# The dense experts of the first layer in two passes over the tokens

## The chip, the cores and the metric

One core of a Trainium2 chip runs the whole program. The metric is device time in microseconds (us), the median of three runs of the kernel. The profile is of one more execution.

## What is computed

4096 tokens (32 samples of 128, width 128, float32) go through two layers; each is a conditioning mixture of experts, a feed-forward part and a residual. The part that matters here is the feed-forward part of the first layer, in which all eight experts run on every token ("dense"):

```python
g = jnp.einsum('bsh,ehf->ebsf', x, w_gate)      # 8 experts, 128 -> 512
u = jnp.einsum('bsh,ehf->ebsf', x, w_up)
h = jax.nn.silu(g) * u
expert_out = jnp.einsum('ebsf,efh->ebsh', h, w_down)
cw = router_probs * gate_weights                # per token and expert
cw = cw / (jnp.sum(cw, axis=-1, keepdims=True) + 1e-09)
out = jnp.einsum('ebsh,bse->bsh', expert_out, cw)
```

The second layer's conditioning part then needs, for each token, the top two of eight router scores of the finished first layer, before its routed experts can be weighted.

## The kernel before

Tokens lie on the free axis in 8 blocks of 512 columns (`BLK`, `NBLK`). Products keep near-float32 precision by splitting both operands into a high part (float32r) and a rest: high x high, low x high, high x low, so three matmuls for each product.

The order of work is one list, `plan()` (lines 91 to 124), of items; the place k of an item is its slot. Kinds: A (shared expert, first layer's conditioning), G (its routed groups), **B** (the dense experts), S and R (shared and routed experts of the second layer), F (its last part). A B item is one block, one expert, one quarter f of the 512 hidden columns; there are 8 experts x 8 blocks x 4 = 256, expert outermost (lines 100 to 102). All engines walk the same slots in order, and every side job is pinned to a slot by a dictionary.

For a B item at slot k, TensorE (PE) multiplies gate and up into two PSUM banks of a ring of four (`up`, lines 917 to 951, six matmuls), and in the same slot does the three down matmuls of the item LAG = 5 slots earlier (`down`, lines 953 to 994). ScalarE (ACT) computes Silu of the gate bank (line 1078). VectorE (DVE) multiplies it with the up bank into `Hf` (line 1551). ACT copies that into the high part `HH` (line 1084), one slot later; DVE, or for every fourth item GpSimd (POOL), subtracts to get the rest `HL` (lines 1571 and 1663). When a block of an expert is done (four items), DVE multiplies its result with the token weights in `CWB` into `TMP` (line 1425), and POOL adds that to the tokens in `XT` (line 1678).

**Expert weights.** `ST` holds two raw experts (`fill_b`, DMA of 768 KB from SyncE's queue, lines 726 on). The split buffers are `WBH`/`WBL`, two of each. `split_wb` pins three pieces of 512 columns for each expert: DVE casts a piece into `WBH` (line 1498), POOL computes the rest `WBL` (line 1605). Piece 0 is gate, 1 is up, 2 is down. The slots, counted from the first slot of an expert, `first_b[ex]`:

```python
first_b = [pos["B", 0, ex, 0].k for ex in range(8)]
fill_b = {pos["G", 8, 0, 0].k: 0, first_b[0] + LAG + 10: 1}
fill_b |= {first_b[ex - 1] + 2: ex for ex in range(2, 8)}
split_wb = {t + 7 + k: (ex, k) for t, ex in fill_b.items() if ex for k in range(3)}
c0 = first_b[1] + LAG + 12
fill_c = {c0: 0, c0 + 1: 1, c0 + 4: 2, c0 + 6: 3}
split_wc = {c0 + 2: (0, 0), c0 + 3: (0, 512), c0 + 4: (1, 0), c0 + 5: (1, 512)}
```

So expert 1 is split at slots 22 to 24 after the first B item, and expert ex at slots 9 to 11 of expert ex - 1, whose pass over the blocks has 32 slots. TensorE waits for each piece in block 0's first item (lines 934 to 936, 984 to 991). `split_wc` splits the second layer's weights in the same way (line 1504) while expert 1 runs, fed by `fill_c`.

**Token weights.** `scr_d` in DRAM holds the weights; after blocks 3 and 7 of an expert SyncE loads those of the next expert, 1 MB each, into `CWB[:, 0]` and `CWB[:, 1]` (lines 749 to 755).

**What follows the B items.** A block that has had its eighth expert is split again for the second layer (`split_b`: ACT line 1030, DVE line 1487). `route_b`, `logit_b` give router scores of blocks 0 to 3. `pick[0]` is a chain of ten steps (`choose`, lines 1328 to 1397) on DVE from slot `lag_b[3] + 1` on, with a Sigmoid on ACT (line 1038) ahead of it; it ends in a transpose on TensorE (line 877), a DMA to DRAM and `gate_slots`: 8 broadcast loads for each block into `CWB` (even blocks) or `ST` and `TMP` (odd blocks), line 658, before R(block) uses them (line 1558). Blocks 4 to 7 have their own chain, `pick[1]`, at item S of block 2.

Of the kernel before, what the change touches and what calls it, by code (L numbers as in the profile page):

```python
# [11 lines left out]
P = 128  # L12
NB = 32
NT = NB * P
BLK = 512
NBLK = NT // BLK
SEG = (0, 42, 86, 128)
LATE = NBLK - 3
LAG = 5
NH = LAG + 1  # L20
NS = 4
# [24 lines left out]
FULL, HALVES = 13, 8  # L46
NGRP = FULL + HALVES
NPAIR = 4 * FULL + 2 * HALVES


def group_order():
# [40 lines left out]
def plan():  # L92
    items = []
    for blk in range(FRONT):
        items += [Item("A", blk, 0, f, f == 3) for f in range(4)]
    for g in range(NGRP):
        items += [Item("G", g, 0, f, f == 3) for f in range(4)]
    for blk in range(FRONT, NBLK):
        items += [Item("A", blk, 0, f, f == 3) for f in range(4)]
    for ex in range(8):  # L100
        for blk in range(NBLK):
            items += [Item("B", blk, ex, f, f == 3) for f in range(4)]

    def shared(blk):
        return [Item("S", blk, f // 2, f % 2, False) for f in range(4)]

    def routed(blk):
        return [Item("R", blk, e, 0, e == 7) for e in range(8)]

    def final(blk):  # L110
        return [Item("F", blk, 0, f, f == 3) for f in range(4)]

    for b in range(0, NBLK, 2):
        items += shared(b) + shared(b + 1)
        for f in (b - 2, b - 1):
            if 0 <= f < LATE:
                items += final(f)
        items += routed(b) + routed(b + 1)
    for b in range(LATE, NBLK):
        items += final(b)  # L120
    return items
# [6 lines left out]
def build(nc, x_d, small_d, pack_d, wa_d, wb_d, wc_d, wf_d, scr_d, wup_d, wdown_d, out_d):  # L128
    with ExitStack() as ctx:
# [3 lines left out]
        def sem(name):  # L133
            return ctx.enter_context(nc.semaphore(name))
# [73 lines left out]
        f_wa = [sem(f"f_wa{i}") for i in range(5)]  # L208
        f_scr = [[sem(f"f_scr{i}{g}") for g in range(2)] for i in range(2)]
        f_cw = [sem("f_cw0"), sem("f_cw1")]  # L210
        f_first = [sem(f"f_first{i}") for i in range(NBLK)]
        f_wex = [sem(f"f_wex{i}") for i in range(4)]
        f_gx, f_gu, f_gd = [[sem(f"{n}{i}") for i in range(NR)] for n in ("f_gx", "f_gu", "f_gd")]
# [47 lines left out]
        def done(kind, blk, ex, f):  # L261
            return pos[kind, blk, ex, f].d
# [51 lines left out]
        split_end = {pos["G", g, 0, 2].k: s for g, s in ((2, (6, 0)), (3, (6, 1)), (7, (7, 0)), (8, (7, 1)))}  # L314

        split_g = {pos["G", g - 1, 0, 2 if g == 2 else 0].k if g else pos["G", 0, 0, 0].k - 1: g for g in range(NGRP)}
        first_b = [pos["B", 0, ex, 0].k for ex in range(8)]
        text = first_b[2]
        fill_b = {pos["G", 8, 0, 0].k: 0, first_b[0] + LAG + 10: 1}
        fill_b |= {first_b[ex - 1] + 2: ex for ex in range(2, 8)}  # L320
        split_wb = {t + 7 + k: (ex, k) for t, ex in fill_b.items() if ex for k in range(3)}
        split_wb |= {pos["G", g, 0, 2].k: (0, k) for k, g in enumerate((12, 13, 15))}
        c0 = first_b[1] + LAG + 12
        fill_c = {c0: 0, c0 + 1: 1, c0 + 4: 2, c0 + 6: 3}
        split_wc = {c0 + 2: (0, 0), c0 + 3: (0, 512), c0 + 4: (1, 0), c0 + 5: (1, 512)}
        split_v1, stack_u2, split_v2 = c0 + 9, c0 + 10, c0 + 11
# [242 lines left out]
        for b in range(NBLK):  # L569
            for ex in range(8):  # L570
                free = pos["R", b - 2, ex, 0].k if b > 1 else done("B", 4 * (ex // 4) + 3, 7, 3)
                if b == 1:
                    free = scr_slots["B", 0] + 1
                gate_slots.setdefault(max(scr_slots["B", b // 4], free) + 1, []).append((b, ex))

        def gate_place(b, ex):
# [24 lines left out]
        def down_weights(it):  # L601
            if it.kind in "AG":
                a = it.f * P
                wh, wl = expert_weights(0 if it.kind == "A" else it.blk % NR + 1, 1)
                return wh[:, a:a + P], wl[:, a:a + P]
            a = 1024 + it.f * P
            return WBH[it.ex % 2][:, a:a + P], WBL[it.ex % 2][:, a:a + P]

        def expert_weights(i, h):

# [21 lines left out]
        def sync_program(e):  # L632
# [12 lines left out]
            for k in range(slots):  # L645
                for b, ex in gate_slots.get(k, []):
                    if b > 1:
                        e.wait_ge(s_gated, n_gated[pos["R", b - 2, ex, 0].n])
                    elif b and ex < 6:
                        e.wait_ge(*st_split(st_fills[ex // 3][-1]))  # L650
                    elif b:
                        e.wait_ge(*acc_done(t_of["B", NBLK - 1, 7]))
                    else:
                        e.wait_ge(s_fin, n_units_ab - 8 + 4 * (ex // 4) + 4)
                    e.wait_ge(f_scr[1][b // 4], 16)
                    src = scr_d[1, b // 4].rearrange("(e t) k -> e (t k)", e=8)[ex][
                        (b % 4) * BLK:(b % 4) * BLK + BLK].partition_broadcast(P)
                    e.dma_start(gate_place(b, ex), src).then_inc(f_gate[b % 2][ex], 16)  # L658
# [53 lines left out]
                if k in fill_b:  # L712
                    ex = fill_b[k]
                    slot = ex % 2
                    if ex > 1:
                        i = st_fills[slot].index(("B", ex))
                        e.wait_ge(*st_split(st_fills[slot][i - 1]))
                        if st_fills[slot][i - 1] == ("C", 3):
                            e.wait_ge(*small.of("fold"))
                            e.wait_ge(s_u2, 4)  # L720
                    elif ex == 1:
                        e.wait_ge(s_wa_lo, 3)
                    else:
                        e.wait_ge(s_wa_lo, 1)
                        e.wait_ge(s_wa0_lo, 1)
                    e.dma_start(ST[:, slot, :], wb_d[ex]).then_inc(f_st[slot], 16)
                if k in turned_b:
                    g = turned_b[k]
                    e.wait_ge(*ab_done.of(("B", "turn", g)))
# [18 lines left out]
                    e.dma_start(out_d[:, b * BLK:b * BLK + BLK], out_place(b)).then_inc(f_out[b], 16)  # L748
                if LAG <= k < len(items) + LAG and items[k - LAG]:
                    it = items[k - LAG]  # L750
                    if it.kind == "B" and it.last and it.blk % 4 == 3 and it.ex < 7:
                        g = it.blk // 4
                        e.wait_ge(s_fin, it.u + 1)
                        src = scr_d[0, g].rearrange("(e t) k -> e (t k)", e=8)[it.ex + 1].partition_broadcast(P)
                        e.dma_start(CWB[:, g, :], src).then_inc(f_cw[g], 16)
            for b in range(NBLK):
                e.wait_ge(f_out[b], 16)

# [139 lines left out]
        def up(e, it):  # L898
            for j, z in enumerate(it.z):
# [15 lines left out]
                if it.kind == "G" and it.f == 0:  # L915
                    e.wait_ge(s_g_hi, it.blk + 1)
                    e.wait_ge(f_gu[it.blk % NR], 16 * (it.blk // NR + 1))
                if it.kind == "B" and it.blk == 0 and it.f == 0:
                    e.wait_ge(*w_hi.of(("B", it.ex, j)))
                if it.kind == "S" and it.blk == 0 and fresh:  # L920
                    e.wait_ge(*w_hi.of("v2"))
                    e.wait_ge(s_u2, 4)
# [9 lines left out]
                e.matmul(o, wh, tokens(it, 0), start=True, stop=False)  # L932
                if it.kind == "A" and it.blk == 0 and it.f == 0:
                    e.wait_ge(s_wa0_lo, 1)
                if it.kind == "B" and it.blk == 0 and it.f == 0:
                    e.wait_ge(*w_lo.of(("B", it.ex, j)))
                e.matmul(o, wl, tokens(it, 0), start=False, stop=False)  # L937
                if fresh and it.kind == "A":
                    if it.blk == 0:
# [13 lines left out]
        def down(e, it):  # L953
# [27 lines left out]
                e.wait_ge(s_wa_hi, 2)  # L981
            if it.kind == "G" and it.f == 0:
                e.wait_ge(f_gd[it.blk % NR], 16 * (it.blk // NR + 1))
            if it.kind == "B" and it.blk == 0 and it.f == 0:
                e.wait_ge(*w_hi.of(("B", it.ex, 2)))
            e.wait_ge(*hi[it.n])
            e.matmul(bk[:, 0:n], wh, HH[:, hs, 0:n], start=it.new, stop=False)  # L987
            if it.kind == "A" and it.blk == 0 and it.f == 0:
                e.wait_ge(s_wa_lo, 1)
            if it.kind == "B" and it.blk == 0 and it.f == 0:  # L990
                e.wait_ge(*w_lo.of(("B", it.ex, 2)))
            e.matmul(bk[:, 0:n], wl, HH[:, hs, 0:n], start=False, stop=False)  # L992
            e.wait_ge(*lo[it.n])
            e.matmul(bk[:, 0:n], wh, HL[:, hs, 0:n], start=False, stop=it.last).then_inc(s_down, 1)  # L994
# [96 lines left out]
        def vector_program(e):  # L1091
# [307 lines left out]
            def finish(it):  # L1399
# [10 lines left out]
                if it.kind == "G":  # L1410
                    n = it.cols
                    if it.blk == 0:
                        e.wait_ge(s_fin, FRONT)
                    e.wait_ge(f_gd[it.blk % NR], 16 * (it.blk // NR + 1))
                    e.wait_ge(s_wm, it.blk + 1)
                    e.scalar_tensor_tensor(out=TMP[:, t % 2, 0:n], in0=bk[:, 0:n], scalar=result_bias(it.blk),
                                           in1=WM[:, it.blk % 2, 0:n], op0=ALU.add, op1=ALU.mult).then_inc(s_fin, 1)
                else:
                    g = it.blk // 4
                    q = CWB[:, g, (it.blk % 4) * BLK:(it.blk % 4) * BLK + BLK]  # L1420
                    if it.ex == 0:
                        e.wait_ge(f_first[it.blk], 16)
                    elif it.blk % 4 == 0:
                        e.wait_ge(f_cw[g], 16 * it.ex)
                    e.tensor_tensor(TMP[:, t % 2, :], bk[:, :], q, ALU.mult).then_inc(s_fin, 1)  # L1425

            e.wait_ge(f_x[0], 16)
# [8 lines left out]
            for k in range(slots):  # L1436
# [52 lines left out]
                if k in split_wb:  # L1489
# [1 line left out]
                    c = slice(j * 512, j * 512 + 512)  # L1491
                    e.wait_ge(f_st[ex % 2], 16 * st_count["B", ex])
                    if ex >= 2:
                        e.wait_ge(s_down, pos["B", NBLK - 1, ex - 2, 3].n + 1)
                    elif ex == 1:
                        e.wait_ge(s_a_lo, NBLK)
                        e.wait_ge(*small.of(("A", 3)))
# [276 lines left out]
```

## Time and profile before

| | us |
|---|---|
| median of 3 runs | 890.34 |
| lowest, highest run | 889.7, 891.0 |
| profiled execution: span, first to last instruction | 886.9 |
| PE busy | 870.3 (98%), 3838 matmuls |
| DVE busy | 682.8 (77%) |
| ACT busy | 574.0 (65%) |
| POOL busy | 402.0 (45%) |

The page gives the profiled execution by its span; the median of the runs is 3.4 us above it, which covers what lies before the first and after the last instruction. Busy matmul times overlap, since matmuls are pipelined: progress of PE is read from the distance between starts. The granted TensorE clock is 1.00 of full speed (2.4 GHz) throughout.

### The profile page before, as it was taken

How to read it: one execution, taken by the hardware profiler on the slowest of the kernel's cores; microseconds unless marked ns; L12 is line 12 of the kernel's file. 1: busy time of each engine (PE TensorE's matmuls, PEld its weight loads, DVE VectorE, ACT ScalarE, POOL GpSimd, SP SyncE). 2: the span in 40 equal slices, each digit the busy share in tenths (PEclk: the TensorE clock that was granted, in tenths of full speed). 3: DMA queues.
4: the chain of work that ended last, by engine and by line, in shares of the span. 5: the costliest groups of instructions: out<-in, count | busy, mean ns of one | idle time of the engine just before them, and what ended most of it. 6: DMA issues, size and time to landing. Idle time of an engine off the chain costs nothing.

```text
span 886.9 us, 12606 instructions
## 1 busy us (share of the span) xinstructions
PE 870.3 (98%) x3838; PEld 690.2 (78%) x3838; DVE 682.8 (77%) x1094; ACT 574.0 (65%) x1029; POOL 402.0 (45%) x376
## 2 busy tenths in 40 slices
PE   8999999999999999999999999999999999999997
PEld 5788888777888888888888888888888777777773
DVE  7877777869689786686686686686665888998887
ACT  7888888765555455555555555555555678989895
POOL 7557783135356453253253252252232227754462
PEclk9999999999999999999999999999999999999999
DMA  9589981023113112012012012011010049582700
GB/s 311 211 276 313 293 295 35 1 86 135 48 48 111 42 42 84 4 45 84 1 48 83 1 48 84 0 48 48 1 48 0 1 108 209 106 178 53 161 25 36
DMA packets 36404, 83.23 MB, mean 94 GB/s; under 512 B 4464, under 2 KB 14320, under 8 KB 34544
## 3 DMA queue, kind: packets, MB, share of 16 engines
q1 hardware_dynamic: 36336, 82.42, 30.1%
q8 instruction: 31, 0.51, 0.2%
q14 instruction: 37, 0.30, 0.1%
HBM read 71.39 MB, written 6.83 MB: 88 GB/s over the span
## 4 chain that ended last, share of the span: by engine, by line
PE 76%; DVE 9%; issue 4%; ACT 3%; SPq 3%; DMA 2%; POOL 1%; DVEq 0%; ACTq 0%; POOLq 0%
PE ps L932 16%; PE ps L951 16%; PE ps L937 16%; PE ps L992 8%; PE ps L994 8%; PE ps L987 8%; DVE HL L1571 3%; SPq L658 1%; PE ps L974 1%; PE ps L972 1%; DVE Hf L1551 1%; DMA ST<-scratch 1%; DVE Hf L1558 1%; ACT HH L1084 1%; SPq L771 1%
## 5 line engine op out<-in xcount | busy, mean ns | idle before, releaser
L1078 ACT ACTIVATE Sg<-ps 128x512 f32<-128x512 f32 x288 | 171.7, 597 | 242.6 <-PE ps L951 242.3
L1551 DVE TENSOR_TENSOR Hf<-ps,Sg 128x512 f32<-128x512 f32 x288 | 197.9, 688 | 147.7 <-ACT Sg L1078 97.5
L1663 POOL TENSOR_TENSOR HL<-Hf,HH 128x512 fp32r<-128x512 f32 x130 | 174.2, 1347 | 157.4 <-ACT HH L1084 141.0
L1084 ACT ACTIVATE HH<-Hf 128x512 fp32r<-128x512 f32 x346 | 216.1, 625 | 21.1 <-DVE Hf L1551 14.4
L1571 DVE TENSOR_TENSOR HL<-Hf,HH 128x512 fp32r<-128x512 f32 x248 | 220.1, 888 | 4.3 <-ACT HH L1084 3.2
L932 PE MATMUL ps<-XHL,WBH 128*128 128x512 f32 x512 | 203.7, 398 | 1.8 <-DVE Hf L1551 1.8
L951 PE MATMUL ps<-XHL,WBH 128*128 128x512 f32 x512 | 202.2, 395 | 0.0
L937 PE MATMUL ps<-XHL,WBL 128*128 128x512 f32 x512 | 202.0, 395 | 0.0
L1678 POOL TENSOR_TENSOR XT<-XT,TMP 128x512 f32<-128x512 f32 x64 | 84.0, 1312 | 248.9 <-DVE TMP L1425 248.7
L932 PEld LDWEIGHTS ps<-XHL,WBH 128*128 128x128 f32 x512 | 96.0, 188 | 27.0 <-DVE Hf L1551 4.0
L951 PEld LDWEIGHTS ps<-XHL,WBH 128*128 128x128 f32 x512 | 96.0, 188 | 23.0
L937 PEld LDWEIGHTS ps<-XHL,WBL 128*128 128x128 f32 x512 | 96.2, 188 | 21.8
L992 PE MATMUL ps<-HH,WBL 128*128 128x512 f32 x256 | 101.0, 395 | 0.0
L987 PE MATMUL ps<-HH,WBH 128*128 128x512 f32 x256 | 100.7, 394 | 0.0
L994 PE MATMUL ps<-HL,WBH 128*128 128x512 f32 x256 | 100.7, 393 | 0.0
L1571 DVE TENSOR_TENSOR HL<-ps,HH 128x512 fp32r<-128x512 f32 (+1 forms) x116 | 69.9, 614 | 30.5 <-ACT HH L1084 29.4
L1071 ACT ACTIVATE ps<-ps,GWU 128x512 f32<-128x512 f32 (+1 forms) x84 | 49.0, 587 | 17.2 <-PE ps L951 17.0
L987 PEld LDWEIGHTS ps<-HH,WBH 128*128 128x128 f32 x256 | 48.0, 187 | 12.0 <-DVE TMP L1425 0.4
L992 PEld LDWEIGHTS ps<-HH,WBL 128*128 128x128 f32 x256 | 48.0, 188 | 11.8
L994 PEld LDWEIGHTS ps<-HL,WBH 128*128 128x128 f32 x256 | 48.1, 188 | 11.2
L932 PE MATMUL ps<-XHL,WCH 128*128 128x512 f32 x128 | 51.2, 400 | 2.0 <-ACT Sg L1078 1.1
L951 PE MATMUL ps<-XHL,WCH 128*128 128x512 f32 x128 | 50.5, 395 | 0.0
(275 smaller groups left out, 1327.6 us busy)
## 6 DMA issues: line engine op xcount, KB each, us to landing
CWB<-scratch SPq DMA_DIRECT2D x14, 1024.0 KB, 4.5
GWD<-expert_down SPq DMA_DIRECT2D x21, 576.5 KB, 4.4
GWU<-expert_up SPq DMA_DIRECT2D x21, 514.0 KB, 5.2
CWB<-scratch SPq DMA_DIRECT2D x40, 256.0 KB, 5.6
ST<-in_wb_dram SPq DMA_DIRECT2D x8, 768.0 KB, 6.2
ST<-scratch SPq DMA_DIRECT2D x24, 256.0 KB, 8.8
GX<-XT SPq DMA_DIRECT2D x68, 64.0 KB, 3.0
XT<-in_x_dram SPq DMA_DIRECT2D x8, 256.0 KB, 5.6
```

The source lines that it names most:

```text
L932: e.matmul(o, wh, tokens(it, 0), start=True, stop=False)
L937: e.matmul(o, wl, tokens(it, 0), start=False, stop=False)
L951: e.matmul(o, wh, tokens(it, 1), start=False, stop=True).then_inc(s_z, 1)
L987: e.matmul(bk[:, 0:n], wh, HH[:, hs, 0:n], start=it.new, stop=False)
L992: e.matmul(bk[:, 0:n], wl, HH[:, hs, 0:n], start=False, stop=False)
L994: e.matmul(bk[:, 0:n], wh, HL[:, hs, 0:n], start=False, stop=it.last).then_inc(s_down, 1)
L1078: e.activation(Sg[:, it.n % NG, :], zb[z % NZ][:, :], ACT.Silu).then_inc(s_act, 1)
L1084: e.activation(HH[:, it.n % NH, 0:it.cols], hidden_place(it), ACT.Copy).then_inc(s_hi_act, 1)
L1551: e.tensor_tensor(Hf[:, it.n % NS, :], zb[z % NZ][:, :], Sg[:, it.n % NG, :], ALU.mult).then_inc(s_prod, 1)
L1571: e.tensor_tensor(l, f, h.bitcast(F32), ALU.subtract).then_inc(s_lo_dve, 1)
L1663: e.tensor_tensor(HL[:, it.n % NH, :], Hf[:, it.n % NS, :], HH[:, it.n % NH, :].bitcast(F32), ALU.subtract).then_inc(s_lo_pool, 1)
L1678: e.tensor_tensor(XT[:, it.blk, :], XT[:, it.blk, :], TMP[:, t % 2, :], ALU.add).then_inc(s_acc, 1)
```

## The change

The B items are made in two passes: blocks 0 to 5 with all eight experts, then blocks 6 and 7 with all eight. An expert has 24 slots in the first pass and 8 in the second. There are 16 turns q instead of 8, so each expert's weights are loaded and split twice. Expert 1 is still split at slots 22 to 24; turns 2 to 8 as before at slots 9 to 11 of the turn ahead; turns 9 to 15 at slots 5 to 7 of the turn ahead. The second layer's weights move from slot 17 to slot 12 of expert 1. Token weights of blocks 6 and 7 are loaded apart. The end of B for blocks 0 to 5, with their splits, router scores and `pick[0]`, falls where the first pass ends, since all those slots are worked out from the items.

```diff
+SPLIT = 6
+PARTS = (range(SPLIT), range(SPLIT, NBLK))
-    for ex in range(8):
-        for blk in range(NBLK):
-            items += [Item("B", blk, ex, f, f == 3) for f in range(4)]
+    for part in PARTS:
+        for ex in range(8):
+            for blk in part:
+                items += [Item("B", blk, ex, f, f == 3) for f in range(4)]
...
-        first_b = [pos["B", 0, ex, 0].k for ex in range(8)]
+        first_b = [pos["B", part[0], ex, 0].k for part in PARTS for ex in range(8)]
...
-        fill_b |= {first_b[ex - 1] + 2: ex for ex in range(2, 8)}
-        split_wb = {t + 7 + k: (ex, k) for t, ex in fill_b.items() if ex for k in range(3)}
+        fill_b |= {first_b[q - 1] + 2: q for q in range(2, 9)}
+        split_wb = {t + 7 + k: (q, k) for t, q in fill_b.items() if q for k in range(3)}
+        fill_b |= {first_b[7] + 12 if q == 9 else first_b[q - 2] + 1: q for q in range(9, 16)}
+        split_wb |= {first_b[q - 1] + LAG + k: (q, k) for q in range(9, 16) for k in range(3)}
...
-        c0 = first_b[1] + LAG + 12
+        c0 = first_b[1] + 12
...
                 if b == 1:
-                    free = scr_slots["B", 0] + 1
+                    free = done("B", NBLK - 1, 7, 3) + 1
...
-                    e.dma_start(ST[:, slot, :], wb_d[ex]).then_inc(f_st[slot], 16)
+                    e.dma_start(ST[:, slot, :], wb_d[ex % 8]).then_inc(f_st[slot], 16)
...
-                    if it.kind == "B" and it.last and it.blk % 4 == 3 and it.ex < 7:
+                    if it.kind == "B" and it.last and it.blk in (3, SPLIT - 1) and it.ex < 7:
                         g = it.blk // 4
+                        n = (it.blk % 4 + 1) * BLK
                         e.wait_ge(s_fin, it.u + 1)
-                        e.dma_start(CWB[:, g, :], src).then_inc(f_cw[g], 16)
+                        e.dma_start(CWB[:, g, 0:n], src).then_inc(f_cw[g], 16)
+                    late = {(SPLIT - 1, 7): 1} | {(NBLK - 1, ex): ex + 2 for ex in range(6)}
+                    if it.kind == "B" and it.last and (it.blk, it.ex) in late:
+                        ex = late[it.blk, it.ex]
+                        a = (2 if ex % 2 == 0 else 0) * BLK
+                        e.wait_ge(s_fin, it.u + 1)
+                        e.dma_start(CWB[:, 1, a:a + 2 * BLK], src).then_inc(f_late[ex % 2], 16)
...
-                if it.kind == "B" and it.blk == 0 and it.f == 0:
-                    e.wait_ge(*w_lo.of(("B", it.ex, j)))
+                if it.kind == "B" and it.blk in (0, SPLIT) and it.f == 0:
+                    e.wait_ge(*w_lo.of(("B", turn_of(it), j)))
...
                     if ex >= 2:
-                        e.wait_ge(s_down, pos["B", NBLK - 1, ex - 2, 3].n + 1)
+                        e.wait_ge(s_down, pos["B", PARTS[(ex - 2) // 8][-1], (ex - 2) % 8, 3].n + 1)
```

## Rows read from the trace of the kernel before

**Rows 1.** The page: span, and part 1 (engine, busy us, share, instructions).
```profile
span 886.9 us, 12606 instructions
PE 870.3 (98%) x3838; PEld 690.2 (78%) x3838; DVE 682.8 (77%) x1094; ACT 574.0 (65%) x1029; POOL 402.0 (45%) x376
```

**Rows 2.** Windows (start:end, length, busy us and instructions), within B and at its end.
```profile
400.00:500.00 100.00, 100.00 (x431) 80.61 (x430) 70.23 (x99) 53.66 (x96) 36.07 (x27) 1.00 0.12 48
690.00:710.00 20.00, 19.22 (x82) 14.48 (x80) 17.68 (x38) 12.27 (x21) 5.91 (x5) 1.00 0.00 0
```

**Rows 3.** Windows of eight B items, without and with a weight split.
```profile
346.00:362.70 16.70, 16.70 (x74) 13.43 (x73) 11.18 (x16) 8.94 (x16) 5.10 (x5) 1.00 0.15 52
449.80:466.50 16.70, 16.70 (x73) 13.47 (x72) 14.79 (x20) 8.95 (x16) 10.14 (x7) 1.00 0.00 1
```

**Rows 4.** Timeline of PE, 684 to 760: start, us, instruction [idle before, releaser].
```profile
695.31 0.50 PE L932 MATMUL ps<-XHL,WBH 128*128 128x512 f32 x1 [0.30 <-DVE Hf L1551]
...
704.48 0.50 PE L932 MATMUL ps<-XHL,WCH 128*128 128x512 f32 x1 [0.49 <-DVE Hf L1551]
...
711.64 0.30 PE L877 MATMUL ps<-sm,q 128*128 128x128 f32 x1 [1.25 <-DVE q L1394]
```

**Rows 5.** Timeline of DVE, 676 to 772.
```profile
687.40 0.69 DVE L1551 TENSOR_TENSOR Hf<-ps,Sg 128x512 f32<-128x512 f32 x1 [1.70 <-ACT Sg L1078]
...
691.91 0.69 DVE L1551 TENSOR_TENSOR Hf<-ps,Sg 128x512 f32<-128x512 f32 x1 [2.29 <-ACT Sg L1078]
...
703.74 0.68 DVE L1551 TENSOR_TENSOR Hf<-ps,Sg 128x512 f32<-128x512 f32 x1
...
711.12 0.38 DVE L1394 TENSOR_TENSOR q<-q 128x128 f32<-128x128 f32 x1
```

**Rows 6.** Timeline of DVE while expert 2 is split, 196 to 320.
```profile
247.07 0.42 DVE L1498 CAST WBH<-ST 128x512 fp32r<-128x512 f32 x1
247.41 0.68 DVE L1551 TENSOR_TENSOR Hf<-ps,Sg 128x512 f32<-128x512 f32 x1
...
249.12 1.52 DVE L1498 CAST WBH<-ST 128x512 fp32r<-128x512 f32 x1
...
251.16 1.15 DVE L1498 CAST WBH<-ST 128x512 fp32r<-128x512 f32 x1
```

**Rows 7.** Timeline of PE in the same stretch.
```profile
250.59 0.40 PE L932 MATMUL ps<-XHL,WBH 128*128 128x512 f32 x1
...
252.92 0.40 PE L937 MATMUL ps<-XHL,WBL 128*128 128x512 f32 x1
```

**Rows 8.** Timeline of POOL: piece 1 of expert 1, piece 1 of expert 2.
```profile
211.13 1.76 POOL L1605 TENSOR_TENSOR WBL<-ST,WBH 128x512 fp32r<-128x512 f32 x1
...
250.72 1.31 POOL L1605 TENSOR_TENSOR WBL<-ST,WBH 128x512 fp32r<-128x512 f32 x1 [0.36 <-DVE WBH L1498]
```

**Rows 9.** Timeline of PE, slot 24 of expert 0.
```profile
211.09 0.39 PE L937 MATMUL ps<-XHL,WBL 128*128 128x512 f32 x1
```

**Rows 10.** Timeline of SyncE's queue (DMA issues), and the page's DMA issues (last: us to landing).
```profile
255.19 0.81 SPq L737 DMA_DIRECT2D ST<-in_wc_dram  x2
...
717.44 6.71 SPq L658 DMA_DIRECT2D CWB<-scratch  x8
...
ST<-in_wc_dram SPq DMA_DIRECT2D x2, 512.0 KB, 3.9
```

**Rows 11.** Timeline of DVE around the second layer's weights.
```profile
259.92 0.69 DVE L1551 TENSOR_TENSOR Hf<-ps,Sg 128x512 f32<-128x512 f32 x1 [1.07 <-ACT Sg L1078]
...
266.20 0.69 DVE L1551 TENSOR_TENSOR Hf<-ps,Sg 128x512 f32<-128x512 f32 x1 [0.36 <-ACT Sg L1078]
266.81 1.41 DVE L1504 CAST WCH<-ST 128x512 fp32r<-128x512 f32 x1
...
276.41 1.28 DVE L1551 TENSOR_TENSOR Hf<-ps,Sg 128x512 f32<-128x512 f32 x2
```

**Rows 12.** Timeline of PE, at the first item S of block 2.
```profile
747.35 0.49 PE L932 MATMUL ps<-XHL,WCH 128*128 128x512 f32 x1 [1.12 <-ACT Sg L1078]
```

More of the change, by code:

```diff
@@ L210, in build @@
         f_cw = [sem("f_cw0"), sem("f_cw1")]
+        f_late = [sem("f_late0"), sem("f_late1")]
         f_first = [sem(f"f_first{i}") for i in range(NBLK)]
@@ L607, in down_weights, with turn_of @@
             return WBH[it.ex % 2][:, a:a + P], WBL[it.ex % 2][:, a:a + P]
+        def turn_of(it):
+            return it.ex + (8 if it.blk >= SPLIT else 0)
         def expert_weights(i, h):
@@ L653, in sync_program @@
                     else:
-                        e.wait_ge(s_fin, n_units_ab - 8 + 4 * (ex // 4) + 4)
+                        e.wait_ge(s_fin, pos["B", 4 * (ex // 4) + 3, 7, 3].u + 1)
                     e.wait_ge(f_scr[1][b // 4], 16)
@@ L750, in sync_program @@
                     it = items[k - LAG]
-                    if it.kind == "B" and it.last and it.blk % 4 == 3 and it.ex < 7:
+                    if it.kind == "B" and it.last and it.blk in (3, SPLIT - 1) and it.ex < 7:
                         g = it.blk // 4
+                        n = (it.blk % 4 + 1) * BLK
                         e.wait_ge(s_fin, it.u + 1)
-                        src = scr_d[0, g].rearrange("(e t) k -> e (t k)", e=8)[it.ex + 1].partition_broadcast(P)
-                        e.dma_start(CWB[:, g, :], src).then_inc(f_cw[g], 16)
+                        src = scr_d[0, g].rearrange("(e t) k -> e (t k)", e=8)[it.ex + 1, 0:n].partition_broadcast(P)
+                        e.dma_start(CWB[:, g, 0:n], src).then_inc(f_cw[g], 16)
[4 more added lines that the diff above has]
+                        e.wait_ge(s_fin, it.u + 1)
+                        src = scr_d[0, 1].rearrange("(e t) k -> e (t k)", e=8)[ex, 2 * BLK:4 * BLK].partition_broadcast(P)
+                        e.dma_start(CWB[:, 1, a:a + 2 * BLK], src).then_inc(f_late[ex % 2], 16)
             for b in range(NBLK):
@@ L917, in up @@
                     e.wait_ge(f_gu[it.blk % NR], 16 * (it.blk // NR + 1))
-                if it.kind == "B" and it.blk == 0 and it.f == 0:
-                    e.wait_ge(*w_hi.of(("B", it.ex, j)))
+                if it.kind == "B" and it.blk in (0, SPLIT) and it.f == 0:
+                    e.wait_ge(*w_hi.of(("B", turn_of(it), j)))
                 if it.kind == "S" and it.blk == 0 and fresh:
@@ L934, in up @@
                     e.wait_ge(s_wa0_lo, 1)
-                if it.kind == "B" and it.blk == 0 and it.f == 0:
-                    e.wait_ge(*w_lo.of(("B", it.ex, j)))
+                if it.kind == "B" and it.blk in (0, SPLIT) and it.f == 0:
+                    e.wait_ge(*w_lo.of(("B", turn_of(it), j)))
                 e.matmul(o, wl, tokens(it, 0), start=False, stop=False)
@@ L983, in down @@
                 e.wait_ge(f_gd[it.blk % NR], 16 * (it.blk // NR + 1))
-            if it.kind == "B" and it.blk == 0 and it.f == 0:
-                e.wait_ge(*w_hi.of(("B", it.ex, 2)))
+            if it.kind == "B" and it.blk in (0, SPLIT) and it.f == 0:
+                e.wait_ge(*w_hi.of(("B", turn_of(it), 2)))
             e.wait_ge(*hi[it.n])
@@ L989, in down @@
                 e.wait_ge(s_wa_lo, 1)
-            if it.kind == "B" and it.blk == 0 and it.f == 0:
-                e.wait_ge(*w_lo.of(("B", it.ex, 2)))
+            if it.kind == "B" and it.blk in (0, SPLIT) and it.f == 0:
+                e.wait_ge(*w_lo.of(("B", turn_of(it), 2)))
             e.matmul(bk[:, 0:n], wl, HH[:, hs, 0:n], start=False, stop=False)
@@ L1419, in finish @@
                     g = it.blk // 4
-                    q = CWB[:, g, (it.blk % 4) * BLK:(it.blk % 4) * BLK + BLK]
+                    a = it.blk % 4 * BLK
+                    if it.blk >= SPLIT:
+                        a = (it.blk - SPLIT + (2 if it.ex % 2 == 0 else 0)) * BLK
+                    q = CWB[:, g, a:a + BLK]
                     if it.ex == 0:
@@ L1424, in finish @@
                         e.wait_ge(f_cw[g], 16 * it.ex)
+                    elif it.blk == SPLIT:
+                        e.wait_ge(f_late[it.ex % 2], 16 * ((it.ex + 1) // 2))
                     e.tensor_tensor(TMP[:, t % 2, :], bk[:, :], q, ALU.mult).then_inc(s_fin, 1)
```

## The prediction

> **What bounds the kernel now.** I read the page first: PE is busy for 870.3 of 886.9 us [rows 1], so the time is TensorE's list of matmuls plus the moments in which it waits. Then the windows by stage: within B, 431 matmuls start in 100 us, one in 0.232 us, at the full granted clock and without a gap [rows 2]; an item of nine matmuls takes 2.09 us, and eight of them 16.7 us. The change moves matmuls and neither adds nor removes one. It can gain only where PE waits today and lose only where it makes PE wait. Third, the timeline of PE from 690 to 712, where the last expert ends and the second layer begins: three waits on DVE, 0.30, 0.49 and 1.25 us idle, 2.04 us in all [rows 4]. With the slower first matmul after each stop they are worth about 2.5 us. They come from `pick[0]`: DVE is busy for 17.7 of 20 us there [rows 2]. Fourth, DVE and POOL where an expert is split, since the change has sixteen turns of that for eight.
>
> How late DVE may be. An item takes two of four PSUM banks, so the second bank of item k + 2 needs the product `Hf` of item k. In the steady state that product starts at 247.41 and is free at about 248.1, and PE wants the bank at 250.59 [rows 6, 7]: DVE may lag by **2.5 us** before PE stops.
>
> What a split costs. Eight items without one keep DVE busy for 11.18 us and POOL for 5.10; with one, 14.79 and 10.14 [rows 3]. So one turn adds **3.6 us** to DVE and 5.0 to POOL. The three casts take 0.42, 1.52 and 1.15 us [rows 6]; the longer two run beside POOL work, as do some slower subtractions. A rule of the Trainium skill bears on this (SBUF — State Buffer, Who interferes with whom): DVE and GpSimd share a port pair as an exclusive lock, a cast can be held up by it, and the second to issue blocks until the first ends. The trace agrees in size, 0.42 against 1.52 us for the same cast. If the lock did not bite where the casts land, three casts at 0.42 us would cost 1.3 us instead of 3.6, and step 3 below would be about 2.3 us smaller.
>
> **The change, part by part.**
>
> Step 1, the start of expert 1. Its pieces stay at slots 22 to 24 after the first B item, but expert 1 now starts at slot 24 instead of 32. In the trace slot 24's second bank takes its low matmul at 211.09 [rows 9]. POOL ends piece 1 at 211.13 + 1.76 = 212.89 [rows 8]. Nothing ahead of this slot changes, so PE waits 212.89 - 211.09 = **1.8 us**. Piece 0 is ready, and piece 2 is only needed five slots later.
>
> Step 2, the second layer's weights, five slots earlier, at slots 14 to 17 of expert 1. SyncE can issue the first load only when expert 2's split has left `ST`, which was at 255.19; it takes 3.9 us to land [rows 10], so 259.1. In the trace DVE's last product before the idle 1.07 us ended at 259.92 - 1.07 = 258.85 [rows 11]; it took 0.7, and slot 14's cast comes ahead of it, so at 258.2. DVE waits 0.9 us, with this slot's product behind it. In the trace the four casts lead from 266.81 to the product at 276.41 [rows 11], 9.6 us, four items on; undisturbed products come every 2.09 us (259.92 to 266.20 are three), so that product should have been at 266.20 + 4 x 2.09 = 274.6: a lag of 1.8 us, under 2.5, and no wait today. From 259.1 the same work ends at 268.7, where 264.1 is due: a lag of 4.6, so PE waits 4.6 - 2.5 = 2.1 us. If the first cast finds POOL idle it takes 0.4 and not 1.4 us, and the wait is 1.1. I take **1.8 us**, nearer the measured sequence; ends: 0 (the load lands in time) and 2.5.
>
> Step 3, the start of the second pass. `pick[0]` starts one slot after the same event as before, 25 slots after the start of the eighth turn, and blocks 4 and 5 are split where they were. The Sigmoid ahead of it already makes DVE late: product at 691.91, where 687.40 + 2.09 = 689.5 was due [rows 5]. DVE then has no idle moment until the last step at 711.12 [rows 5], and PE pays 2.5 us. In the change the same chain stands there with three casts for turn 9 in slots 5 to 7 of turn 8, in the middle of it. On an engine with no slack the 3.6 us go straight through; a cast may take the place of an idle moment elsewhere, so I take **3.5 us** more (ends 1.3, all casts short, and 4.5). PE meets it first at the weights of turn 9. Today the product of the slot with the second cast starts at 703.74, where 687.40 + 6 x 2.09 and some 0.3 us of router matmuls make 700.2 due [rows 5], 3.5 us late. With two casts of 1.1 ahead of it, it is 5.7 late; piece 1 has 0.9 us to spare (step 4) and a little under 1 more, as the cast here begins later in its slot, so PE waits about 3.9 us there, and at the end of the chain the total has grown to 6. They are one delay, not two. The waits of [rows 4] are not saved: they move to this place.
>
> Step 4, the seven turns 9 to 15. Split slots 5 to 7 of 8 keep the distance of three slots to the first use. In the trace, POOL ends piece 1 at 250.72 + 1.31 = 252.03 [rows 8], and three slots after the split begins PE would use it at 252.92 [rows 7]: 0.9 us to spare. DVE needs 14.8 of 16.7 us per turn, POOL 10.1 [rows 3], so neither falls behind. I cost this at **0**. The cover is that 0.9 us; if DVE starts a turn more than 0.9 us late, PE waits for the difference.
>
> Step 5, edits at nothing. Weight loads: 6.3 MB more, with twelve slots (25 us) between issue and use, on queues moving 48 GB/s in this stage [rows 2]. Token weights: seven loads of 1 MB become fourteen of 0.5 MB; each has about 12 slots. In SyncE's order nothing that is due soon stands behind the new waits. The cast's new wait for the down matmuls of the turn before is for matmuls that PE issues in the slot before.
>
> Step 6, what gets easier. The gates of block 0 for experts 0 to 3 are loaded during the second pass. At the end 12 loads are left of 16; eight took 6.7 us to issue from 717.44 on [rows 10]. Block 1's gates come 3 to 4 us earlier. DVE waits hardly for them today, but the ACT table switches behind R(1) cost PE 1.12 us at 747.35 [rows 12] and may start a little earlier: **-0.4 us** (ends 0 and -1.3).
>
> Sum: 1.8 + 1.8 + 3.5 + 0 - 0.4 = +6.7 us. The profiled execution would have a span of 886.9 + 6.7 = 893.6; the median stands 3.4 us above the span, so 890.3 + 6.7 = **897.0 us**.
>
> **The rivals.** A measurement of this kernel can tell about 0.2% (1.8 us) from no change.
>
> Rival A, the chain is hidden: in the second pass PE has 134 us of work behind `pick[0]`, the three waits of [rows 4] vanish and the new splits hide. Then -2.5 - 0.4, 887.4 us; with step 1 alone, 889.2. For it: POOL is idle for over half of the time, and DVE for 30% in B [rows 2]. Against it: PE has no reserve to use later, for its banks hold only two items, so a late DVE stops it at once, wherever the chain stands; and steps 1 and 2 come from fixed slots. Chance 0.14.
>
> Rival B, every turn of the second pass is late. It sits at piece 1 of each new turn and decides once DVE or POOL is over 0.9 us behind at slot 5. If each of seven turns misses by 1 us, +7: 904 us. For it: 89% of DVE is used, and the rest must absorb order effects. Against it: the six splits from turn 2 on in the trace look alike, and DVE is free again by slot 14 (idle before 259.92 [rows 11]), five slots after the split began. Chance 0.16.
>
> Rival C, only the fixed slots cost: the casts of turn 9 fall in gaps of the longer stretch, and step 2's load lands in time. 1.8 + 1.3 - 0.4 = +2.7: 893.0 us. Chance 0.15.
>
> **How the numbers follow.** My forecast has 0.55. The range takes in C and most of B: low 890.5, which leaves out most of A, and high 903, above the sum with all upper ends, 1.8 + 2.5 + 4.5 = +8.8 (899.1), and one half of B. Faster by over 1.8 us: A without step 1, 0.09. Within 1.8 us: the rest of A and the low end of C, 0.07. Slower: 0.84.
>
> **What the profile of the changed kernel would show.** PE matmuls still 3838; DVE busy near 682.8 + 8 x 3.6 = 712 us, POOL near 402 + 40 = 442. Step 1: at line 937 PE idle for about 1.8 us near 211, released by POOL WBL. Step 2: waits on Hf near 261 to 270. Step 3: near 565 to 585 some 6 us of waits, on WBL, Hf and line 1394, and none at the end of B. Step 4: no wait on WBL in the later turns. If there are such waits, B holds; if the waits near 565 to 585 are under 3 us, step 3 is wrong and the change may end level.

## The result, and the profile after

The changed kernel took 896.66 us (median of 4 runs, 895.52 to 898.57), the kernel before 890.67 beside it: ratio 1.0072, 95% interval 1.0057 to 1.0086, so **6.0 us slower**. The forecast was 897.0.

Page of the changed kernel, span and part 1, the group of part 5 that has the new work, and part 6:

```profile
span 894.5 us, 12708 instructions
...
PE 874.0 (98%) x3838; PEld 692.1 (77%) x3838; DVE 712.9 (80%) x1118; ACT 574.2 (64%) x1029; POOL 441.0 (49%) x400
...
L1631 POOL TENSOR_TENSOR WBL<-ST,WBH 128x512 fp32r<-128x512 f32 x48 | 74.7, 1556 | 10.4 <-DVE WBH L1524 10.4
...
ST<-in_wb_dram SPq DMA_DIRECT2D x16, 768.0 KB, 5.9
...
CWB<-scratch SPq DMA_DIRECT2D x7, 1024.0 KB, 4.6
CWB<-scratch SPq DMA_DIRECT2D x14, 512.0 KB, 3.6
```

PE has the same 3838 matmuls as in [rows 1]. DVE gained 30.1 us and POOL 39.0, for 24 more casts and 24 more subtractions. What is lost shows in PE's timeline (start, us, instruction, idle before and its releaser). All its waits of 0.25 us or more between the first dense item and item S of block 2, but two, near 173 and 204, that the kernel before has too:

```profile
214.29 0.50 PE L958 MATMUL ps<-XHL,WBL 128*128 128x512 f32 x1 [1.67 <-POOL WBL L1631]
...
254.27 0.50 PE L953 MATMUL ps<-XHL,WBH 128*128 128x512 f32 x1 [0.25 <-DVE Hf L1577]
...
263.24 0.50 PE L953 MATMUL ps<-XHL,WBH 128*128 128x512 f32 x1 [0.34 <-DVE Hf L1577]
...
582.37 0.50 PE L953 MATMUL ps<-XHL,WBH 128*128 128x512 f32 x1 [0.29 <-DVE Hf L1577]
...
593.09 0.69 PE L953 MATMUL ps<-XHL,WBH 128*128 128x512 f32 x1 [1.61 <-DVE Hf L1577]
...
602.43 0.30 PE L898 MATMUL ps<-sm,q 128*128 128x128 f32 x1 [1.73 <-DVE q L1415]
...
754.76 0.50 PE L953 MATMUL ps<-XHL,WCH 128*128 128x512 f32 x1 [0.77 <-ACT Sg L1099]
```

The first is expert 1's piece 1, the next two the second layer's weights, then three for the router chain at the start of the second pass, the counterpart of [rows 4], and the last answers to [rows 12]. At the end of the dense items, where [rows 4] lie, PE no longer waits.

What these cost is read from the starts. I compared the start of the n-th up group (line 932 before, 953 after) in both traces; the amount by which the changed kernel is later:

| place | later by, us | gained there |
|---|---|---|
| expert 0, slot 22 | 1.37 | 1.37 (ahead of the B items) |
| expert 1 under way | 3.2 to 3.3 | 1.8 to 1.9 |
| rest of the first pass | 4.34 | 1.1 |
| second layer, S of blocks 0 and 1 | 7.77 | 3.43 |
| S and R of blocks 2 on | 7.38 | -0.39 |

The first 1.37 us lie in the first 60 us, which the change does not touch; they differ from one execution to the next (-0.2 to 2.2 us in the profiles of the experiments below). From the first split on it is 1.8 + 1.1 + 3.4 - 0.4 = 6.0 us, the difference of the medians.

### The profile page after: what moved, and what is told of

It reads as the page before. It is cut to its first block, busy times and chain, and to the rows that moved or that the text cites. A ratio compares the mean times of both kernels' runs of the same rounds, so it can differ in the third digit from the quotient of the medians.

```text
span 894.5 us, 12708 instructions
## 1 busy us (share of the span) xinstructions
PE 874.0 (98%) x3838; PEld 692.1 (77%) x3838; DVE 712.9 (80%) x1118; ACT 574.2 (64%) x1029; POOL 441.0 (49%) x400
## 4 chain that ended last, share of the span: by engine, by line
PE 80%; DVE 9%; ACT 4%; issue 3%; POOL 2%; DMA 1%; DVEq 0%; SPq 0%; ACTq 0%; POOLq 0%
PE ps L953 17%; PE ps L958 16%; PE ps L972 16%; PE ps L1013 8%; PE ps L1015 8%; PE ps L1008 8%; DVE HL L1597 3%; PE ps L995 2%; PE ps L993 1%; DVE Hf L1577 1%; DVE Hf L1584 1%; ACT HH L1105 1%; POOL HL L1689 1%; DVE HH L1594 1%; PE ps L988 1%
## 5 line engine op out<-in xcount | busy, mean ns | idle before, releaser
L1597 DVE TENSOR_TENSOR HL<-Hf,HH 128x512 fp32r<-128x512 f32 x248 | 229.8, 927 | 4.4 <-ACT HH L1105 3.2
L1631 POOL TENSOR_TENSOR WBL<-ST,WBH 128x512 fp32r<-128x512 f32 x48 | 74.7, 1556 | 10.4 <-DVE WBH L1524 10.4
L953 PE MATMUL ps<-XHL,WCH 128*128 128x512 f32 x128 | 50.9, 398 | 1.2 <-ACT Sg L1099 0.8
```

The source lines that it names most:

```text
L1597: e.tensor_tensor(l, f, h.bitcast(F32), ALU.subtract).then_inc(s_lo_dve, 1)
```

## The experiments

All but the last three were timed in five rounds beside the kernel before, whose median was 889.7 there. The changed kernel's ratio of 1.0072 was taken in its own comparison. Half-intervals are about 0.13%, 1.2 us, and a difference of two ratios carries about 0.2%, 1.7 us. So steps of 1 to 2 us are not told by the times alone: for them the trace is the witness and the ratio its companion. The last three kernels (e9, e10, e11) were run once each, for their profiles.

| kernel | median, us | ratio to before | interval |
|---|---|---|---|
| changed kernel | 896.66 | 1.0072 | 1.0057 to 1.0086 |
| e1, expert 1 split a slot earlier | 894.57 | 1.0053 | 1.0039 to 1.0066 |
| e2, layer-2 weights 3 slots later | 895.61 | 1.0069 | 1.0055 to 1.0082 |
| e7, the same 1 slot later | 894.73 | 1.0056 | 1.0042 to 1.0069 |
| e3, router chain spread | 891.09 | 1.0019 | 1.0010 to 1.0028 |
| e4, turn 9 not split | 891.84 | 1.0028 | 1.0012 to 1.0043 |
| e6, turns 10 to 15 a slot late | 903.15 | 1.0149 | 1.0134 to 1.0164 |
| e8, before, with a ninth split | 894.21 | 1.0045 | 1.0032 to 1.0058 |
| **e5, e1, e7 and e3 together** | **887.55** | **0.9972** | 0.9961 to 0.9984 |

### e1: expert 1 split one slot earlier

```diff
-        split_wb = {t + 7 + k: (q, k) for t, q in fill_b.items() if q for k in range(3)}
+        split_wb = {t + (6 if q == 1 else 7) + k: (q, k) for t, q in fill_b.items() if q for k in range(3)}
```

> The changed kernel with the three pieces of expert 1 split one slot earlier (slots 21 to 23 of expert 0 instead of 22 to 24). Theory (the fixed slots are late by 1.8 us for an expert that now starts at slot 24): the wait of TensorE on POOL's WBL at line 958, 1.67 us idle near 214, disappears, since a slot is 2.1 us; about -1.8 us against the changed kernel, 894.9. Rival (DVE is saturated there, so the casts only push another product): the wait moves to Hf and the time stays at 896.7.

The time fell by 0.19% (1.7 us). In its timeline PE has one wait from 200 to 216, the one that is older than the change, and none on WBL:

```profile
204.15 0.50 PE L953 MATMUL ps<-XHL,WBH 128*128 128x512 f32 x1 [0.67 <-DVE Hf L1577]
```

So the loss was one of slots, and the casts did not push a product instead. The 1.7 us are at the edge of what the times can tell; that the wait is gone is what shows the cause.

### e2 and e7: the second layer's weights later

```diff
-        c0 = first_b[1] + 12
+        c0 = first_b[1] + 15      # e2
+        c0 = first_b[1] + 13      # e7
```

> The changed kernel with the second layer's weights three slots later (slot 15 of expert 1 instead of 12). Theory (they stand too close behind expert 2's split: DVE waited 0.77 us for the first load and carried that lag on): the waits of TensorE near 254, 263 and 272 go, about -1.1 us against the changed kernel, 895.6. Rival (the waits come from POOL holding the port, whatever the slot): 896.7.

e2 gained next to nothing in time, and by the starts it loses 0.6 us more than the changed kernel in this stretch. The two waits at the casts went, and one of 1.42 us came. DVE's timeline, then that of SyncE's queue:

```profile
268.67 0.43 DVE L1533 CAST V1S<-ST 128x512 fp32r<-128x512 f32 x1 [3.10 <-DMA ST<-in_wf_dram]
```
```profile
261.33 0.33 SPq L768 DMA_DIRECT2D CWB<-scratch  x1
261.70 0.43 SPq L753 DMA_DIRECT2D ST<-in_wf_dram  x1
```

The load of the fourth part (line 753) is pinned to slot 21 and now stands behind the token weights' load of slot 20, which waits until block 3's result is finished. DVE needs the load at slot 24 and stood 3.10 us for it. My expectation had looked at DVE alone, and not at what the moved step passes in SyncE's queue.

> The changed kernel with the second layer's weights one slot later (13 instead of 12 of expert 1), so that the load of the fourth part still stands ahead of the token weights' load in SyncE's queue; three slots later it stood behind it, DVE waited 3.1 us for it and the gain was lost. Theory: DVE no longer waits for the first load, TensorE's waits near 254 and 263 shrink to 0.3 us or less, about -0.7 us. Rival (the casts themselves are too dense): no change.

With one slot, the load stays ahead of slot 20. PE has no wait from 216 to 300 at all; -0.16% (1.4 us), within what the times can tell; by the starts the stretch costs nothing now, 1.1 us less than in the changed kernel. The theory holds, and the rivals of both (the casts or the port, whatever the slot) fall.

### e3: the router chain spread

```diff
-        pick = [[lag_b[3] + 1 + i for i in (0, 1, 2, 3, 5, 6, 7, 8, 10, 11)],
+        pick = [[lag_b[3] + i for i in (10, 18, 20, 26, 28, 34, 36, 42, 44, 45)],
```

> The changed kernel with the ten steps of the first router chain spread over the second pass, from its slot 10 to 45, away from the split slots. Theory (at the start of the second pass chain, block splits and three casts together overload DVE): the waits near 582 to 602, 6.0 us in all with the slow matmuls behind the long one, go but for some 0.5; about -5.5 us against the changed kernel, 891.2, level with the kernel before. Rival (PE has no reserve, so the chain costs its 2.5 us wherever it stands, only the collision goes): -3.5 us, 893.2.

-0.53% (4.7 us). PE's waits from 540 to 745, in which the changed kernel idled 3.63 us in three:

```profile
630.70 0.50 PE L953 MATMUL ps<-XHL,WBH 128*128 128x512 f32 x1 [0.15 <-DVE Hf L1577]
...
648.62 0.50 PE L953 MATMUL ps<-XHL,WBH 128*128 128x512 f32 x1 [0.62 <-DVE Hf L1577]
...
665.47 0.30 PE L898 MATMUL ps<-sm,q 128*128 128x128 f32 x1 [0.57 <-DVE q L1415]
```

Three short waits are left, 1.34 us idle, each where a step of the chain comes three slots after a split's last cast. The time, 4.7 us, lies between the theory (5.5) and the rival (3.5), and its noise does not part them. By the starts, part of what the chain cost before is saved (0.9 us of some 2.5), so the rival (2.5 us wherever it stands) fails in part here, and wholly with e5, where the steps behind a split stand four slots after it and no wait is left. A step must also keep clear of the recovery from the split before it.

### e4: turn 9 not split

```diff
+                    if ex == 9:
+                        c = slice(j * 512, j * 512 + 8)
```

(for the cast and for the subtraction; expert 1's weights are left out for blocks 6 and 7)

> The changed kernel with turn 9's three casts and three subtractions cut to 8 columns each; expert 1's weights are left out for blocks 6 and 7. Theory (the casts of turn 9 are what the second pass adds to the chain): the waits fall back to the 2.5 us that the chain cost before, -3.5 us against the changed kernel, 893.2. Rival (the move of the chain itself made it worse): under -1 us, 896.

-0.44% (3.9 us). Its waits near 581 to 598 stand beside [rows 4]:

```profile
581.46 0.50 PE L953 MATMUL ps<-XHL,WBH 128*128 128x512 f32 x1 [0.30 <-DVE Hf L1579]
...
590.72 0.50 PE L953 MATMUL ps<-XHL,WBH 128*128 128x512 f32 x1 [0.57 <-DVE Hf L1579]
...
593.38 0.50 PE L953 MATMUL ps<-XHL,WBH 128*128 128x512 f32 x1 [0.30 <-DVE Hf L1579]
...
598.37 0.30 PE L898 MATMUL ps<-sm,q 128*128 128x128 f32 x1 [1.23 <-DVE q L1415]
```

2.40 us idle for 2.04 before, and by the starts 0.25 us more than before: without turn 9's split the chain costs about what it cost at its old place. The move alone saves nothing.

### e8: the collision in the old order

```diff
+        fill_b[first_b[7] + 12] = 8
+        split_wb |= {first_b[7] + 29 + k: (8, k) for k in range(3)}
```

> The kernel before with one more expert loaded and split, unused, in slots 29 to 31 after the start of expert 7: the place in the router chain at which the change splits turn 9. Theory (three casts on a saturated DVE cost what they take, whatever the order of blocks): +3.5 us against the kernel before, ratio 1.0039. Rival (the collision needs the second pass, with B items instead of S items): +1 us or less.

+0.45% (4.0 us). Nothing of the two passes is in this kernel; an unused split at the same point of the chain is enough:

```profile
695.72 0.50 PE L934 MATMUL ps<-XHL,WBH 128*128 128x512 f32 x1 [0.30 <-DVE Hf L1553]
...
706.43 0.50 PE L934 MATMUL ps<-XHL,WCH 128*128 128x512 f32 x1 [1.92 <-DVE Hf L1553]
...
710.10 0.50 PE L934 MATMUL ps<-XHL,WCH 128*128 128x512 f32 x1 [1.32 <-DVE Hf L1553]
...
715.78 0.30 PE L879 MATMUL ps<-sm,q 128*128 128x128 f32 x1 [1.93 <-DVE q L1396]
```

5.47 us idle for 2.04 in [rows 4], +3.4, and 3.7 by the starts, beside the 3.6 us of DVE work that [rows 3] give for a split. With e4 this shows the cause from both sides.

### e6: how wide the margin of the later turns is

```diff
-        split_wb |= {first_b[q - 1] + LAG + k: (q, k) for q in range(9, 16) for k in range(3)}
+        split_wb |= {first_b[q - 1] + LAG + k + (q > 9): (q, k) for q in range(9, 16) for k in range(3)}
```

> The changed kernel with turns 10 to 15 split one slot later (slots 6 to 8 of the turn ahead instead of 5 to 7). Theory (piece 1 has 0.9 us to spare, and a slot is 2.1 us): TensorE waits about 1.2 us on POOL's WBL at each of six turns, +7 us against the changed kernel, 903. Rival (DVE and POOL are nearer to their limit than the margin shows): more than 2 us a turn, +12 or more; or, if the margin is larger than read, no change.

903.15 us, +0.77% (6.9 us). Two of its six waits on WBL:

```profile
615.55 0.50 PE L958 MATMUL ps<-XHL,WBL 128*128 128x512 f32 x1 [0.95 <-POOL WBL L1631]
...
633.51 0.50 PE L958 MATMUL ps<-XHL,WBL 128*128 128x512 f32 x1 [0.94 <-POOL WBL L1631]
```

The matmul that waits starts 1.1 us late, the one behind it 1.2, and 6 x 1.2 = 7.2. A slot of 2.1 less 1.1 is a margin of 1.0; read beforehand it was 0.9. One slot is the difference between nothing and 7 us.

### e5: all three mended

```diff
+        split_wb = {t + (6 if q == 1 else 7) + k: (q, k) for t, q in fill_b.items() if q for k in range(3)}
+        c0 = first_b[1] + 13
+        pick = [[lag_b[3] + i for i in (11, 19, 20, 27, 28, 35, 36, 43, 46, 47)],
```

> The changed kernel with all three mended: expert 1 split one slot earlier, the second layer's weights one slot later (slot 13 of expert 1), the first router chain spread over slots 11 to 47 of the second pass. Theory (the three losses are separate and each is one of slots): -1.8 - 0.7 - 5.3 us against the changed kernel, and the 2.5 us that the chain cost before are saved with it, so about 1.8 us under the kernel before, ratio 0.998. Rival (extra DVE work of 3.6 us for each of eight turns is paid somewhere): ratio 1.002 or more.

887.55 us, ratio 0.9972 (0.9961 to 0.9984): 2.5 us **under the kernel before** (2.2 by the medians), and 8.9 under the changed one (0.9972 against 1.0072). A window over most of B and the start of the second layer (busy us of PE, PEld, DVE, ACT, POOL), and the page's part 1:

```profile
205.00:745.00 540.00, 540.00 (x2355) 436.36 (x2354) 436.50 (x622) 302.32 (x535) 256.92 (x188) 1.00 0.21 66
```
```profile
PE 871.8 (98%) x3838; PEld 692.1 (78%) x3838; DVE 711.7 (80%) x1118; ACT 575.1 (65%) x1029; POOL 443.6 (50%) x400
```

PE does not wait once in 540 us. The extra 29 us on DVE are all still there, and PE pays for none of them: the rival, that they must be paid somewhere, falls.

### e9, e11 and e10: the gates of block 0, and a second look at the kernel before

> The changed kernel with all gate loads of block 0 after the last dense block, so that 16 loads stand there as before and not 12. Theory (earlier gates let the ACT table switches start earlier): the wait of TensorE on ACT Sg near 754 grows from 0.77 back to about 1.1 us, and DVE waits for a DMA into TMP again. Rival (it is not the gates): 0.77 us as in the changed kernel.

Its wait was 0.77 us as in the changed kernel, but this proves nothing: the edit moved the slots of the loads and no wait, and SyncE issued four of the eight loads near 692, some 33 us ahead. e11 adds the wait:

```diff
-                        e.wait_ge(s_fin, pos["B", 4 * (ex // 4) + 3, 7, 3].u + 1)
+                        e.wait_ge(s_fin, pos["B", NBLK - 1, 7, 3].u + 1)
```

> The changed kernel with all eight gate loads of block 0 made to wait for the last dense block (the run before this one only moved their slots, and SyncE's queue still issued four of them 33 us ahead, so it did not test this). Theory (earlier gates let the ACT table switches start earlier): 16 loads in a row, DVE waits for a DMA into TMP and TensorE's wait on ACT Sg near 754 grows from 0.77 to about 1.1 us. Rival (it is not the gates): 0.77 us.

PE and DVE of e11:

```profile
756.10 0.50 PE L955 MATMUL ps<-XHL,WCH 128*128 128x512 f32 x1 [1.22 <-ACT Sg L1101]
```
```profile
745.49 0.69 DVE L1586 TENSOR_TENSOR Hf<-ps,ST 128x512 f32<-128x512 f32 x1 [0.79 <-DMA ST<-scratch]
```

The wait is back. The DMA that DVE waited for was into ST, not TMP.

> The kernel before once more, for a second profile. Theory: its wait on ACT Sg at the first item S of block 2 is 1.1 us again, and its three waits of the router chain are 0.30, 0.49 and 1.25 us again. Rival: the 1.1 us varies from run to run, and 0.8 is seen.

The second profile of the kernel before repeats [rows 4] and [rows 12]: 0.31, 0.49, 1.25 and 1.16 us. One thing does not fit: e8 has all 16 loads late and waited only 0.79 us there. So in the changed kernel earlier gates take this wait from 1.2 to 0.8 us, as far as one profile with late loads can show (the other profiles with four early loads have 0.74 to 0.77); what else does is open.

## Why the prediction was right

**The sum** was +6.7, measured 6.0, and the three places were the right ones. Its translation to a median was lucky: the text took the median to be 3.4 us above the span. In the profiled run of the changed kernel the time is 2.1 us above the span (896.6 and 894.5), in the second look at the kernel before 1.8 (888.71 and 886.9). The 3.4 mixed one execution with the median of others; comparing spans alone would have given +7.6, with 1.4 us of start-up that is no effect.

**Step 1**, 1.8 us: measured 1.83 in the starts, 1.67 idle, released by POOL WBL; e1 removes it. This is what a trace does best: a fixed event, and a consumer moved to a known place.

**Step 2**, 1.8 us: measured 1.1. DVE's wait for the first load was 0.77 where 0.9 was read:

```profile
245.53 0.43 DVE L1530 CAST WCH<-ST 128x512 fp32r<-128x512 f32 x1 [0.77 <-DMA ST<-in_wc_dram]
```

The cast behind it took 0.43 and not 1.41, the short case of the text, for which it gave 1.1 us. From this cast to the product four items on it was 8.0 us (245.53 to 253.54) where the text took 9.6. But the casts account for only 0.5 of the 1.1; the other 0.6 came at 263, behind the low-rank weights (line 1533), which the text had not priced. So its short case met the total by luck. Six other profiles with these slots (e1, e3, e4, e6, e9, e11) lose 0.8 to 1.0 us here, and none of them has the wait of 0.25 us near 254.

**Step 3**, 3.5 us: measured 3.43, e4 and e8 showing the same from two sides. The text's intermediate stage failed: it had PE wait 3.9 us for the weights of turn 9 first. In the changed kernel the product held PE (593.09) for 1.61 us, and the weights would have held it for about a quarter of a microsecond more, as they did at this place in e1, e2, e6 and e9 (0.24 to 0.25 us). One part of the gap is read from DVE: from 578.97, the product behind the idle 2.29 us, to 592.35 below it took 13.38 us, and before, from 691.91 to 703.74 [rows 5], 11.83. The two casts ahead of this product made it 1.55 us later and not the 2.2 of the text; the rest of the gap is open. At the end of the chain (601.91, before 711.12) DVE is 3.7 us later than before, and that sets the total. The place was misread as well: the text looked for the waits between 565 and 585, and they stand at 582 to 602. Its own sign of error, under 3 us of waits in 565 to 585, would have fired with 0.29 us there, though the step was right.

**The rule on the shared port** applied, in a way that the text missed. In this stretch, DVE and then POOL of the changed kernel:

```profile
578.97 0.69 DVE L1577 TENSOR_TENSOR Hf<-ps,Sg 128x512 f32<-128x512 f32 x1 [2.29 <-ACT Sg L1099]
...
589.47 1.38 DVE L1387 TENSOR_TENSOR q<-q,sm 128x128 f32<-128x128 f32 x1
...
592.01 0.42 DVE L1524 CAST WBH<-ST 128x512 fp32r<-128x512 f32 x1
592.35 0.68 DVE L1577 TENSOR_TENSOR Hf<-ps,Sg 128x512 f32<-128x512 f32 x1
592.95 0.98 DVE L1394 TENSOR_TENSOR q<-q 128x128 f32<-128x128 f32 x1
593.96 1.25 DVE L1396 TENSOR_TENSOR q<-q 128x128 f32<-128x128 f32 x1
...
595.65 0.42 DVE L1524 CAST WBH<-ST 128x512 fp32r<-128x512 f32 x1
```
```profile
588.96 1.73 POOL L1631 TENSOR_TENSOR WBL<-ST,WBH 128x512 fp32r<-128x512 f32 x1
...
592.51 1.27 POOL L1631 TENSOR_TENSOR WBL<-ST,WBH 128x512 fp32r<-128x512 f32 x1 [1.82 <-DVE WBH L1524]
593.74 1.33 POOL L1689 TENSOR_TENSOR HL<-Hf,HH 128x512 fp32r<-128x512 f32 x1
...
596.16 1.30 POOL L1631 TENSOR_TENSOR WBL<-ST,WBH 128x512 fp32r<-128x512 f32 x1 [1.09 <-DVE WBH L1524]
```

The casts were all short, 0.42 us, the case for which the text gave 1.3 us. The cost of 3.4 us came nonetheless. Small operations of the chain took 1.38, 0.98 and 1.25 us, where the same three took 0.28, 0.77 and 0.29 before. Each ended 0.14 to 0.16 us after a subtraction of POOL: the first two after those of the split (590.69 and 593.78), the third after the one for the tokens' product (line 1689, 595.07), which POOL made right behind the second. The Trainium skill (SBUF — State Buffer, Who interferes with whom) says that a DVE instruction with two SBUF inputs is locked out too while GpSimd reads SBUF. These times agree with it, and so do the same three operations in e8 (1.38, 0.99 and 1.27 us) and in e4 (0.29, 1.17 and 0.29), though e4 cuts casts and subtractions together and no run takes POOL's work away alone. So short casts did not make this split cheap: what POOL did was paid for by the operations that stood beside it. The lower end of step 3 was wrongly placed.

**Step 4**, 0 us: right. No turn after turn 9 made PE wait, and POOL ran as in [rows 8]; PE used the piece, done at 613.05, 0.9 us later:

```profile
611.75 1.30 POOL L1631 TENSOR_TENSOR WBL<-ST,WBH 128x512 fp32r<-128x512 f32 x1 [0.36 <-DVE WBH L1524]
```
```profile
613.94 0.39 PE L958 MATMUL ps<-XHL,WBL 128*128 128x512 f32 x1
```

Rival B was 1 us away, as e6 shows. **Step 5**, 0: right, no wait on a weight or token load in the second pass. **Step 6**, -0.4: measured -0.39. e11 supports the cause in its sign only: by the starts it comes out of this place 0.9 us later than the changed kernel, where 0.4 was to be explained.

**Rival A** was right that the second pass can hide the chain, and its objection in the text, that a late DVE stops PE wherever the chain stands, holds for a chain in one piece only. Spread out, it is hidden: e5 stands at 887.55 where A said 887.4. The change left that gain lying, as it moved the chain with its old spacing next to a new split.

## What to carry to other kernels

When a schedule is pinned to slots, price a reordering by slots: for each pinned job the distance to its new consumer, then each queue that a moved job passes. In this kernel DVE, 77 to 80% busy, took 29 us more at no cost once each burst had room to be worked off before the next (e5), and cost 3.4 to 3.7 us for one burst that hadn't (e8): the backlog against the consumer's reserve (here 2.5 us) decided, and not the busy share.

## What was not expected of the hardware

After the wait of 1.61 us the granted clock fell. Windows (last but two: clock) and PE's starts:

```profile
590.00:594.00 4.00, 2.29 (x7) 0.84 (x6) 3.90 (x8) 2.08 (x5) 2.18 (x3) 0.90 0.06 23
594.00:597.00 3.00, 3.00 (x8) 2.37 (x9) 2.93 (x6) 0.47 (x2) 1.91 (x2) 0.56 0.00 0
597.00:603.00 6.00, 4.27 (x19) 3.20 (x19) 5.90 (x13) 2.16 (x5) 1.73 (x2) 1.00 0.42 131
```
```profile
594.85 0.63 PE L1008 MATMUL ps<-HH,WBH 128*128 128x512 f32 x1
595.28 0.63 PE L1013 MATMUL ps<-HH,WBL 128*128 128x512 f32 x1
```

Matmuls start 0.43 us apart where 0.23 is usual, and from 594 to 596 the granted clock is 0.50, so 1.2 GHz for some seven of them, about 1.5 us. Here it was hidden, as DVE was late anyway: e9, without it, loses as much in this stretch, 6.1 us by the starts between slots that the kernel before reaches at 580 and 600. In the profiles of e1, e2 and e6 it came behind the last wait instead, where nothing hid it; e1 and e2 lose 7.6 us there. e6's profile therefore holds about 1.5 us that are not its six waits. All four runs of the changed kernel have a mean clock of 0.995 to 0.998, those of e5 0.999 to 1.000. But e8 waited 1.92 and 1.93 us and shows no such run of slow matmuls. e9 has the same waits as e1, to 0.01 us (1.61, 0.24, 0.81 and 1.93), and in a window of 20 us over them the clock does not fall:

```profile
588.00:608.00 20.00, 15.35 (x62) 10.90 (x61) 18.92 (x34) 8.89 (x16) 9.04 (x7) 1.00 0.20 69
```

So the waits alone do not decide it; what does is open.
